# A two-layer attention kernel on one core: the last batch's stacks and rows of maxima on two queues, its value projections in the score banks

## The chip, the core and the metric

The kernel runs on 1 core of one Trainium2 chip. The metric is the device time in microseconds; lower is better. Engines are named as in the profile: PE (TensorE), DVE (VectorE), ACT (ScalarE), POOL (GpSimd), SP (SyncE, which here only issues DMAs). ACT issues DMAs too, from the same in-order list as its computations.

## The reference, cut to what matters

`x` is (16, 256, 512): 16 batches of 256 channels by 512 tokens. Two residual layers follow each other.

```python
def _L0_cond_ref(x, mask, Wq, Wo):             # 8 heads of 32, 512 tokens
    qh = heads(transpose(x) @ Wq.T)
    logits = (scale * qh @ qh^T * cmask + (1.0 - cmask) * NEG) * rmask
    ctx = softmax(logits) @ qh
    return transpose(ctx @ Wo.T)

def _L1_cond_ref(x, emb, W_emb, b_emb, g_norm, W_qkv, g_q, g_k, W_out):   # 16 heads of 32, 256 rows of 512
    scale, shift = split(emb @ W_emb + b_emb)
    xn = _rms_norm(x, g_norm) * (1.0 + scale) + shift
    q, k, v = split(xn @ W_qkv)
    q, k = _rms_norm(q, g_q), _rms_norm(k, g_k)
    o = softmax(q @ k^T * d ** (-0.5)) @ v
    return o + o @ W_out

x = x + _L0_cond_ref(x, cond, ...)
x = x + _L1_cond_ref(x, cond, ...)
```

## The kernel before

**The pipeline.** The program on each engine is a list of iterations, i = -1 to 17. A steady iteration does layer 0 of batch i (score steps A and B), layer 1 of batch i - 1 (steps C) and the output projection of batch i - 2. The engines meet by semaphores alone; on each engine the order is the one written out in the lists. Iterations 0 and 1, 15, 16 and 17 have lists of their own. **Iteration 16 is the one that the change touches**: no layer 0 is left there; it holds layer 1 of batch 15 and the output projection of batch 14 (`out1(i, i - 2, ...)`).

**Layer 1 of a batch, in its order.** `qk` (L598) projects queries and keys, `take_heads` and `square_heads` on ACT, `square_sums` and `add_eps` on DVE, `power_heads` on POOL (L2269) and `norm_heads` make the RMS norm. `heads_rows` (L616) transposes the heads on PE into four banks of PM. `round_heads` on ACT (L1317) rounds them to KQHI, `split1` on DVE (L1926) puts the remainder into KQLO and frees the bank. Scores are taken as a matmul over 97 rows: three stacked copies of 32 rows (high, low, high against high, high, low) and a row with the maxima. **A stack** is the six DMAs, 128 KB each, that copy these rows of one head of each group of four into A1 and B1 (`stack1_rows`); all of a stack's DMAs wait until the four banks are freed, so until `split1` 3. `maxima1` (L472) on PE and on DVE (L1826) find the maxima of 4 groups c = 0 to 3; in the last batch `rows1_half` transposes them in two halves on PE into PO (L488), ACT copies each half to NMT1 and issues four DMAs (L1281) that put them into row 96 of B1. `score1(c, h)` (L517), `exp1(c, h)` (L1217), `add_keys1` on POOL (L2287), `values_and_sums1(c)` (L552, L555), `take_context1`, `invert1` (L1934), `context1` (L1941) and `out1` (L632) follow; a score waits for the exponential two before it, since there are two score banks PS.

**Values.** `values1(i, t, ...)` (L598, V<-PX on ACT) projects the values of row block t. The argument list names the steps of the contraction, c = 0 to 3; each step is one product, two instructions in the trace, and the same holds for the steps of `out1`. Its result lies in PX, the bank of the order `BIG`, whose users wait for each other's evacuation by `big_taken`.

**The end of batch 14.** `out1(16, 14, t)` writes PX; `residual1` on DVE (L1947) adds PX to X1R and frees PX; `store` on SP (L2455) writes the two halves of X1R out (256 KB each, one after each residual). `keep_x1` on ACT copies X1, the residual of batch 15, into the same X1R. It waits for both stores:

```python
            def keep_x1(i, b):
                act.wait_ge(stored.sem, stored.at(b - 1))
                copy(X1R[:, :, :], X1[:, :, :]).then_inc(x1r_done.sem, 1)
```

In the list of ACT for iteration 16 `keep_x1` stands between `exp1(1, 3)` and `exp1(2, 0)`. In that of DVE `residual1(14, 0)` stands between `split1` 0 and `split1` 1, and `residual1(14, 1)` between the first and second `maxima1`. SP has stacks 0, 1 and 2, ACT has stack 3.

## Time and profile before

| | us |
|---|---|
| median of 3 runs | 1301.64 |
| lowest, highest | 1295.12, 1302.73 |
| the profiled execution | 1301.46 |
| its span | 1299.3 |
| mean granted clock of PE over the span | 0.974 |

The median is of separate executions; all rows are of the one profiled execution, whose span starts with its first instruction. The last batch's layer 1 takes the span's last 66 us, from about 1233 on.

### The profile page before, as it was taken

How to read it: one execution, taken by the hardware profiler on the slowest of the kernel's cores; microseconds unless marked ns; L12 is line 12 of the kernel's file. 1: busy time of each engine (PE TensorE's matmuls, PEld its weight loads, DVE VectorE, ACT ScalarE, POOL GpSimd, SP SyncE). 2: the span in 40 equal slices, each digit the busy share in tenths (PEclk: the TensorE clock that was granted, in tenths of full speed). 3: DMA queues.
4: the chain of work that ended last, by engine and by line, in shares of the span. 5: the costliest groups of instructions: out<-in, count | busy, mean ns of one | idle time of the engine just before them, and what ended most of it. 6: DMA issues, size and time to landing. Idle time of an engine off the chain costs nothing.

```text
span 1299.3 us, 20729 instructions
## 1 busy us (share of the span) xinstructions
PE 1239.1 (95%) x6769; PEld 579.9 (45%) x6769; DVE 1034.5 (80%) x920; ACT 768.6 (59%) x1394; POOL 770.4 (59%) x387
## 2 busy tenths in 40 slices
PE   6959899999999999999999999999999999999998
PEld 4314344544445454444545444454544444454434
DVE  5665878888887887888788788878878887887764
ACT  1525566665656666565666666566665656666623
POOL 1235648376665838666583866658385765837542
PEclk7778999999999999999999999999999999999999
DMA  7153543437354433636344363634336263433432
GB/s 211 38 191 90 114 115 81 108 85 169 83 134 108 107 102 92 160 82 139 105 102 107 94 157 82 147 98 104 103 100 150 83 152 93 112 99 72 103 70 60
DMA packets 77976, 143.00 MB, mean 110 GB/s; under 512 B 21553, under 2 KB 23089, under 8 KB 77873
## 3 DMA queue, kind: packets, MB, share of 16 engines
q1 hardware_dynamic: 69552, 130.36, 40.1%
q10 hardware_dynamic: 8320, 11.32, 3.3%
q8 instruction: 58, 0.95, 0.3%
q14 instruction: 46, 0.37, 0.1%
HBM read 32.02 MB, written 8.39 MB: 31 GB/s over the span
## 4 chain that ended last, share of the span: by engine, by line
PE 75%; POOL 7%; DVE 5%; SPq 4%; issue 4%; ACT 3%; DMA 1%; ACTq 1%; DVEq 0%; POOLq 0%
PE PX L598 24%; PE PS L500 8%; PE PO L530 7%; PE PX L632 7%; PE PS L517 5%; POOL RQK L2269 5%; PE PO L552 5%; SPq L2450 4%; PE PM L463 4%; PE PX L569 2%; PE PM L569 2%; PE PO L555 2%; PE PM L472 2%; PE PM L541 1%; PE PM L580 1%
## 5 line engine op out<-in xcount | busy, mean ns | idle before, releaser
L1210 ACT ACTIVATE E<-PS,KBIAS 128x512 f32<-128x512 f32 x512 | 340.8, 686 | 191.0 <-PE PS L500 150.0
L598 PE MATMUL PX<-WQKV,XNT 128*128 128x512 f32 x752 | 379.4, 607 | 1.3 <-ACT XNT L1354 0.8
L1819 DVE TENSOR_REDUCE NM<-PM 128x4 f32<-128x2048 f32 x128 | 292.0, 2282 | 73.9 <-PE PM L463 73.7
L2257 POOL TENSOR_TENSOR E<-E 128x1024 f32<-128x1024 f32 x112 | 262.8, 2366 | 95.8 <-PE PO L530 93.0
L500 PE MATMUL PS<-B,A 97*128 97x512 f32 x512 | 289.5, 600 | 3.4 <-ACT E L1210 2.7
L2287 POOL TENSOR_TENSOR KQLO<-E 128x1024 f32<-128x1024 f32 x64 | 151.5, 2368 | 227.3 <-ACT E L1217 225.7
L2269 POOL TENSOR_TENSOR RQK<-RQK,HALF 128x16 f32<-128x16 f32 x64 | 214.3, 3354 | 96.5 <-DVE RQK L1907 96.2
L1217 ACT ACTIVATE E<-PS 128x512 f32<-128x512 f32 x256 | 146.7, 597 | 111.5 <-PE PS L517 110.9
L598 PEld LDWEIGHTS PX<-WQKV,XNT 128*128 128x128 f32 x752 | 134.9, 192 | 99.3 <-issue 89.8
L1826 DVE TENSOR_REDUCE NM<-PM 128x8 f32<-128x2048 f32 x64 | 146.4, 2288 | 37.9 <-PE PM L472 37.9
L500 PEld LDWEIGHTS PS<-B,A 97*128 97x128 f32 x512 | 93.0, 191 | 158.1 <-issue 108.3
L517 PE MATMUL PS<-B,A 97*128 97x256 f32 x512 | 135.1, 371 | 5.2 <-ACT E L1217 2.5
L530 PE MATMUL PO<-E,V 128*32 128x512 f32 x1024 | 135.7, 613 | 1.4 <-ACT E L1210 1.4
L632 PE MATMUL PX<-WOUT,OT 128*128 128x512 f32 x248 | 126.3, 601 | 0.2 <-DVE OT L1941 0.2
L1934 DVE RECIPROCAL T<-T 128x256 f32<-128x256 f32 x64 | 111.5, 1742 | 12.1 <-ACT T L1188 12.1
L517 PEld LDWEIGHTS PS<-B,A 97*128 97x128 f32 x512 | 80.6, 190 | 82.4 <-issue 65.9
L1837 DVE TENSOR_TENSOR E<-E 128x1024 f32<-128x1024 f32 x80 | 102.8, 1286 | 16.9 <-ACT E L1210 15.4
L1857 DVE RECIPROCAL R<-R 128x256 f32<-128x256 f32 x64 | 109.6, 1735 | 1.0
L1188 ACT ACTIVATE QK<-PX 128x512 f32<-128x512 f32 x62 | 37.1, 599 | 75.7 <-PE PX L598 75.7
L463 PE MATMUL PM<-QHI 32*128 32x512 f32 x512 | 66.8, 510 | 13.0 <-DVE NM L1819 9.6
L1900 DVE TENSOR_REDUCE SSQ<-YSQ 128x16 f32<-128x512 f32 x64 | 43.7, 683 | 40.3 <-ACT YSQ L1301 40.3
L448 PE MATMUL PX<-XB,WQ 128*128 128x512 f32 x128 | 63.8, 622 | 7.2 <-DMA XB<-x 6.4
(87 smaller groups left out, 1354.6 us busy)
## 6 DMA issues: line engine op xcount, KB each, us to landing
A<-KQHI SPq DMA_DIRECT2D x126, 128.0 KB, 2.4
B<-KQHI SPq DMA_DIRECT2D x126, 128.0 KB, 2.5
A<-QHI SPq DMA_DIRECT2D x248, 64.0 KB, 2.0
B<-QHI SPq DMA_DIRECT2D x248, 64.0 KB, 2.0
XB<-x SPq DMA_DIRECT2D x16, 512.0 KB, 4.2
X<-x ACTq DMA_DIRECT2D x16, 512.0 KB, 5.0
out<-X1R SPq DMA_DIRECT2D x32, 256.0 KB, 2.9
A<-KQLO SPq DMA_DIRECT2D x63, 128.0 KB, 2.4
```

The costliest lines, as they stand in the source:

```text
L500: mm(PS[n % 2][:, :], A0[0:97, h, g * P:(g + 1) * P], B0[0:97, h, :], start=True, stop=True).then_inc(score_full, 1)
L517: last = mm(PS[n % 2][:, kb * N1:(kb + 1) * N1], A1[0:97, hq, c, kb * P:(kb + 1) * P], B1[0:97, hq, c, :], start=True, stop=True)
L530: last = mm(PO[h * DH:(h + 1) * DH, :], V0[:, q, g, h * DH:(h + 1) * DH], E[:, probs(seg, i, g), h, :], start=(g == 0), stop=(g == KB0 - 1))
L598: last = mm(bank, XNT[:, c, t * P:(t + 1) * P], WQKV[:, c, part * DM:(part + 1) * DM], start=(c == 0), stop=(c == 3))
L632: last = mm(bank, OT[:, c, t * P:(t + 1) * P], WOUT[:, c, :], start=(c == 0), stop=(c == 3))
L1210: fn(E[:, probs(seg, i, g), h, :], PS[n % 2][:, :], ACT.Exp, bias=KBIAS[:, g, b:b + 1], scale=SCALE).then_inc(exp_done, 1)
L1217: fn(E[:, probs("C", i, c), h, :], PS[n % 2][:, :], ACT.Exp, scale=SCALE_RAW).then_inc(exp_done, 1)
L1819: v.tensor_reduce(NM0[:, q, :].rearrange("p (h k) -> p h k", k=KB0)[:, :, kb], PM[:, :, :], axis=AX.X, op=ALU.max, negate=True).then_inc(m ...
L1826: v.tensor_reduce(maxima_rows(b)[:, c // 2, c % 2, :, :], PM[:, :, :].rearrange("p h (a k) -> p h a k", a=2), axis=AX.X, op=ALU.max, negat ...
L2257: g_.tensor_tensor(running(seg, i)[:, heads_, :], running(seg, i)[:, heads_, :], E[:, probs(seg, i, g), heads_, :], ALU.add).then_inc(done, 1)
L2269: g_.tensor_tensor(rqk, rqk, HALF[:, :], ALU.pow).then_inc(rqk_done.sem, 1)
L2287: g_.tensor_tensor(key_sums(c), e[:, :, 0:N1], e[:, :, N1:2 * N1], ALU.add).then_inc(esum_done.sem, 1)
```

## The change

It has four parts, all in iteration 16.

1. Stack 1 moves from SP to ACT: SP issues stacks 0 and 2, ACT stacks 1 and 3. Of the four DMAs of a half of the maxima (`half_rows`), ACT issues the first two and SP the last two, behind a wait for ACT's copy.
2. The value projections of batch 15 go to the banks of its first two scores (`last_values_bank`), which are free there; ACT counts their copies in a new semaphore `values_taken`, for which scores 0 and 1 and the first context wait. They leave the order `BIG`.
3. PE's list: value projections move forward, in between the transposes and the maxima; the steps of `out1(14, 0)` and `out1(14, 1)` move back behind them, the last two of `out1(14, 1)` in between the scores.
4. ACT's list takes both copies of V ahead of the first exponential and half 1 of the maxima behind the second; DVE's list takes `residual1(14, 1)` behind the fourth maxima.

```diff
         16: (
             (("p0", 0), 1, 0), (("p0", 1), 1, 0), (("w0", 0), 0, 0), (("p1", 0), -1, 0), (("p1", 2), -1, 0),
-            (("w1", 0), -2, 0), (("w1", 1), -2, 0), (("v1", 0), -1, 0), (("v1", 1), -1, 0)),
+            (("w1", 0), -2, 0), (("w1", 1), -2, 0)),
...
+        def half_rows(j):
+            return [(B1[96:97, h, 2 * j:2 * j + 2, :].rearrange("p c (k t) -> p (c k) t", t=P).bitcast(F32),
+                     NMT1[h * QH:(h + 1) * QH, j, :].bitcast(F32)) for h in range(QH)]
+
+        def last_values_bank(t):
+
+            return PS[SCORES.upto(("C", t), NB) % 2]
...
                 if b == NB - 1:
+                    if u < 2:
+                        pe.wait_ge(values_taken, u + 1)
...
                 if c == 0:
-                    pe.wait_ge(big_taken, BIG.upto(("v1", 1), i))
+                    if b == NB - 1:
+                        pe.wait_ge(values_taken, 2)
+                    else:
+                        pe.wait_ge(big_taken, BIG.upto(("v1", 1), i))
...
-                bank = heads_bank(i - 1, k) if key[0] == "p1" else PX[:, :]
+                late = key[0] == "v1" and i == NB
+                bank = last_values_bank(t)[:, :] if late else heads_bank(i - 1, k) if key[0] == "p1" else PX[:, :]
                 if cs[0] == 0:
-                    if key[0] == "p1" and i == NB and k % 2:
+                    if late:
+                        pe.wait_ge(exp_done, SCORES.ahead(("C", 0), i))
+                    elif key[0] == "p1" and i == NB and k % 2:
...
@@ PE, iteration_16
                 heads_rows(i, i - 1, 0)
                 heads_rows(i, i - 1, 1)
-                out1(i, i - 2, 0, 3)
+                values1(i, 0, 0)
                 heads_rows(i, i - 1, 2)
                 heads_rows(i, i - 1, 3)
-                out1(i, i - 2, 1, 0, 1)
+                out1(i, i - 2, 0, 3)
+                values1(i, 0, 1)
                 maxima1(i, i - 1, 0)
...
                 score1(i, i - 1, 1, 0)
                 score1(i, i - 1, 1, 1)
-                values1(i, 1, 1, 2, 3)
+                out1(i, i - 2, 1, 2)
                 score1(i, i - 1, 1, 2)
                 score1(i, i - 1, 1, 3)
+                out1(i, i - 2, 1, 3)
...
@@ ACT
-                for h in range(QH):
-                    act.dma_start(B1[96:97, h, 2 * j:2 * j + 2, :].rearrange("p c (k t) -> p (c k) t", t=P).bitcast(F32),
-                                  NMT1[h * QH:(h + 1) * QH, j, :].bitcast(F32)).then_inc(row1_half_in[j], 16)
+                for dst, src in half_rows(j)[:2]:
+                    act.dma_start(dst, src).then_inc(row1_half_in[j], 16)
...
                 round_heads(i, i - 1, 3)
+                stack1(i, i - 1, 1)
                 stack1(i, i - 1, 3)
                 rows1_half(i, i - 1, 0)
                 values1(i, i - 1, 0)
+                values1(i, i - 1, 1)
                 exp1(i, i - 1, 0, 0)
                 exp1(i, i - 1, 0, 1)
+                rows1_half(i, i - 1, 1)
                 exp1(i, i - 1, 0, 2)
                 exp1(i, i - 1, 0, 3)
-                rows1_half(i, i - 1, 1)
                 exp1(i, i - 1, 1, 0)
                 exp1(i, i - 1, 1, 1)
-                values1(i, i - 1, 1)
...
@@ DVE, iteration_16
                 maxima1(i, i - 1, 0)
-                residual1(i, i - 2, 1)
                 maxima1(i, i - 1, 1)
                 maxima1(i, i - 1, 2)
                 maxima1(i, i - 1, 3)
+                residual1(i, i - 2, 1)
...
@@ SP
+            def rows1_half(i, b, j):
+                sp.wait_ge(context_taken, CONTEXT_TAKEN.upto(("n1", j), i))
+                for dst, src in half_rows(j)[2:]:
+                    sp.dma_start(dst, src).then_inc(row1_half_in[j], 16)
...
             def iteration_16(i):
                 stack1(i, i - 1, 0)
-                stack1(i, i - 1, 1)
                 stack1(i, i - 1, 2)
+                rows1_half(i, i - 1, 0)
+                rows1_half(i, i - 1, 1)
                 store(i, i - 2)
```

What the lists become, at three places. Lines are those of each file; in the changed one `heads_rows` is L633, `out1` L649, `values1` L615, `maxima1` L481, `score1` L528, `rows1_half` L497 on PE.

PE from the second pair of head transposes to the first maxima, before:

```order
L616 MATMUL PM<-IDENT,QK 128x128 [waits bank_taken2,max_done,qn_done]
L616 MATMUL PM<-IDENT,QK 128x128 x3
L632 MATMUL PX<-WOUT,OT 128x512 [waits ot_done]
L616 MATMUL PM<-IDENT,QK 128x128 [waits bank_taken0,max_done,qn_done]
L616 MATMUL PM<-IDENT,QK 128x128 x3
L616 MATMUL PM<-IDENT,QK 128x128 [waits bank_taken1,max_done,qn_done]
L616 MATMUL PM<-IDENT,QK 128x128 x3
L632 MATMUL PX<-WOUT,OT 128x512 [waits ot_done,big_taken]
L632 MATMUL PX<-WOUT,OT 128x512 [waits ot_done]
L472 MATMUL PM<-KQHI 128x256 [waits bank_taken2,bank_taken3,bank_taken1,kqhi_done,bank_taken0,max_done]
L472 MATMUL PM<-KQHI 128x256 x7
```

and now:

```order
L633 MATMUL PM<-IDENT,QK 128x128 [waits bank_taken2,max_done,qn_done]
L633 MATMUL PM<-IDENT,QK 128x128 x3
L615 MATMUL PS1<-WQKV,XNT 128x512 [waits exp_done]
L633 MATMUL PM<-IDENT,QK 128x128 [waits bank_taken0,max_done,qn_done]
L633 MATMUL PM<-IDENT,QK 128x128 x3
L633 MATMUL PM<-IDENT,QK 128x128 [waits bank_taken1,max_done,qn_done]
L633 MATMUL PM<-IDENT,QK 128x128 x3
L649 MATMUL PX<-WOUT,OT 128x512 [waits ot_done]
L615 MATMUL PS1<-WQKV,XNT 128x512
L481 MATMUL PM<-KQHI 128x256 [waits bank_taken2,bank_taken3,bank_taken1,kqhi_done,bank_taken0,max_done]
L481 MATMUL PM<-KQHI 128x256 x7
```

The last step of `out1(14, 0)` stood ahead of the second pair of transposes and now stands behind it; a step of the values has its place.

PE at the second group of scores up to the first of the third, before:

```order
L517 MATMUL PS1<-B1,A1 128x256 [waits exp_done]
L517 MATMUL PS1<-B1,A1 128x256
L517 MATMUL PS0<-B1,A1 128x256 [waits exp_done]
L517 MATMUL PS0<-B1,A1 128x256
L598 MATMUL PX<-WQKV,XNT 128x512 x3
L517 MATMUL PS1<-B1,A1 128x256 [waits exp_done]
L517 MATMUL PS1<-B1,A1 128x256
L517 MATMUL PS0<-B1,A1 128x256 [waits exp_done]
L517 MATMUL PS0<-B1,A1 128x256
L517 MATMUL PS1<-B1,A1 128x256 [waits exp_done,row1_half_in1]
L517 MATMUL PS1<-B1,A1 128x256
```

and now:

```order
L528 MATMUL PS1<-B1,A1 128x256 [waits exp_done]
L528 MATMUL PS1<-B1,A1 128x256
L528 MATMUL PS0<-B1,A1 128x256 [waits exp_done]
L528 MATMUL PS0<-B1,A1 128x256
L649 MATMUL PX<-WOUT,OT 128x512 [waits ot_done]
L528 MATMUL PS1<-B1,A1 128x256 [waits exp_done]
L528 MATMUL PS1<-B1,A1 128x256
L528 MATMUL PS0<-B1,A1 128x256 [waits exp_done]
L528 MATMUL PS0<-B1,A1 128x256
L649 MATMUL PX<-WOUT,OT 128x512 [waits ot_done]
L528 MATMUL PS1<-B1,A1 128x256 [waits exp_done,row1_half_in1]
L528 MATMUL PS1<-B1,A1 128x256
```

The three steps of the values are gone from between the scores, and one step of `out1(14, 1)` stands behind the second score of the group, the last one behind the fourth.

ACT from stack 3 to the first exponentials, before:

```order
L1231 DMA A1<-KQHI 32x1024 [waits bank_taken1,bank_taken0,score_full,bank_taken2]
L1231 DMA A1<-KQLO 32x1024
L1231 DMA A1<-KQHI 32x1024
L1231 DMA B1<-KQHI 32x1024 x2
L1231 DMA B1<-KQLO 32x1024
L1188 ACTIVATE NMT1<-PO 16x128 [waits row1_in,n1_half0]
L1281 DMA B1<-NMT1 1x4x128 [waits context_taken]
L1281 DMA B1<-NMT1 1x4x128 x3
L1188 ACTIVATE V1<-PX 128x512 [waits visit_done,v1_full]
L1217 ACTIVATE E<-PS1 128x512 [waits score_full,visit_done]
L1217 ACTIVATE E<-PS0 128x512 [waits score_full]
```

and now, from the second DMA of stack 3, which has all of stack 1 ahead of it:

```order
L1253 DMA A1<-KQLO 32x1024
L1253 DMA A1<-KQHI 32x1024
L1253 DMA B1<-KQHI 32x1024 x2
L1253 DMA B1<-KQLO 32x1024
L1210 ACTIVATE NMT1<-PO 16x128 [waits row1_in,n1_half0]
L1303 DMA B1<-NMT1 1x4x128 [waits context_taken]
L1303 DMA B1<-NMT1 1x4x128
L1210 ACTIVATE V1<-PS1 128x512 [waits visit_done,v1_full]
L1210 ACTIVATE V1<-PS0 128x512 [waits visit_done,v1_full]
L1239 ACTIVATE E<-PS1 128x512 [waits score_full,visit_done]
L1239 ACTIVATE E<-PS0 128x512 [waits score_full]
```

The copy of the maxima's half 0 has six more DMA issues ahead of it, two instead of four behind it, and both copies of V are ahead of the first exponential.

## Rows read from the trace of the kernel before

**Rows 1.** The page: its header, and the chain's shares by engine.

```profile
span 1299.3 us, 20729 instructions
...
PE 75%; POOL 7%; DVE 5%; SPq 4%; issue 4%; ACT 3%; DMA 1%; ACTq 1%; DVEq 0%; POOLq 0%
```

**Rows 2.** The chain that ended last, in time: start us, us, what.

```profile
1256.25 0.51 SPq L2450
...
1267.85 3.68 DMA B<-KQLO
...
1295.27 0.87 PE PM L632 x2
1296.17 0.69 DVE X1R L1947
```

**Rows 3.** Timeline, 1251 to 1256: start, us, engine, line, operation, count [idle before].

```profile
1251.72 1.12 PE L632 MATMUL PX<-WOUT,OT 128*128 128x512 f32 x2 [0.18 <-DVE OT L1941]
...
1253.45 0.68 DVE L1947 TENSOR_TENSOR X1R<-PX,X1R 128x512 f32<-128x512 f32 x1
...
1254.04 2.06 DVE L1926 SCALAR_TENSOR_TENSOR KQLO<-PM,GQK,KQHI 128x512 fp32r<-128x512 f32 x3
...
1254.18 1.98 PE L632 MATMUL PX<-WOUT,OT 128*128 128x512 f32 x4
```

**Rows 4.** Timeline: the last issue of ACT's stack; the first of SP's second.

```profile
1259.89 0.69 ACTq L1231 DMA_DIRECT2D B<-KQLO  x1
...
1260.42 0.56 SPq L2450 DMA_DIRECT2D A<-KQHI  x1
```

**Rows 5.** Stretches: length, busy PE, PEld, DVE, ACT, POOL, PEclk, DMA share, GB/s.

```profile
1203.00:1209.00 6.00, 5.84 (x34) 2.19 (x26) 5.98 (x5) 3.21 (x5) 6.00 (x3) 1.00 0.92 201
...
1256.00:1258.00 2.00, 1.85 (x12) 1.01 (x12) 1.17 (x2) 0.00 (x0) 0.00 (x0) 1.00 0.33 66
1258.00:1260.00 2.00, 1.35 (x11) 0.42 (x10) 1.99 (x3) 0.00 (x0) 0.00 (x0) 1.00 0.97 275
1260.00:1262.00 2.00, 1.01 (x2) 0.18 (x2) 2.00 (x1) 0.00 (x0) 0.00 (x0) 0.99 1.07 246
1262.00:1264.00 2.00, 1.72 (x10) 1.12 (x11) 0.66 (x2) 0.27 (x1) 0.00 (x0) 0.50 1.05 219
...
1268.00:1270.00 2.00, 1.55 (x3) 0.48 (x4) 2.00 (x1) 0.57 (x1) 0.00 (x0) 0.80 1.03 235
...
1272.00:1274.00 2.00, 2.00 (x7) 0.99 (x5) 0.00 (x0) 1.22 (x3) 0.63 (x1) 0.55 0.07 15
```

**Rows 6.** DMA issues, median us to landing: batch 15's stacks (two), batch 14's (last).

```profile
A<-KQHI SPq DMA_DIRECT2D x6, 128.0 KB, 4.2
...
B<-KQLO ACTq DMA_DIRECT2D x1, 128.0 KB, 5.4
...
A<-KQHI SPq DMA_DIRECT2D x8, 128.0 KB, 2.4
```

**Rows 7.** Timeline of ACT, 1262 to 1282.

```profile
1262.98 3.06 ACTq L1281 DMA_DIRECT2D B<-NMT  x4
...
1273.09 0.25 ACT L1188 ACTIVATE NMT<-PO 16x128 fp32r<-16x128 f32 x1
1273.37 2.42 ACTq L1281 DMA_DIRECT2D B<-NMT  x4
1275.89 1.09 ACT L1217 ACTIVATE E<-PS 128x512 f32<-128x512 f32 x2 [2.55 <-PE PS L517]
...
1279.47 1.07 ACT L1188 ACTIVATE X1R<-X 128x1024 f32<-128x1024 f32 x1
1280.42 1.10 ACT L1217 ACTIVATE E<-PS 128x512 f32<-128x512 f32 x2
```

**Rows 8.** Timeline: PE's first scores, two scores of group 2, SP's last stores.

```profile
1269.84 0.71 PE L517 MATMUL PS<-B,A 97*128 97x256 f32 x4 [0.45 <-issue]
...
1279.26 0.90 PE L517 MATMUL PS<-B,A 97*128 97x256 f32 x4 [0.80 <-ACT E L1217]
...
1296.10 1.12 SPq L2455 DMA_DIRECT2D out<-X1R  x2
```

More of the change, by code:

```diff
@@ L363, in cond_resid @@
         big_taken = sem("big_taken")
+        values_taken = sem("values_taken")
         def running(seg, i):
@@ L433, in keep_warm @@
                 for _ in range(n):
-                    mm(PO[:, P:2 * P], IDENT[:, :], IDENT[:, :], start=True, stop=True)
+                    mm(PS[1][:, 0:P], IDENT[:, :], IDENT[:, :], start=True, stop=True)
             def quad_free(key, i):
@@ L1131, in iteration_16 @@
                 heads_rows(i, i - 1, 1)
-                out1(i, i - 2, 0, 3)
+                values1(i, 0, 0)
                 heads_rows(i, i - 1, 2)
                 heads_rows(i, i - 1, 3)
-                out1(i, i - 2, 1, 0, 1)
+                out1(i, i - 2, 0, 3)
+                values1(i, 0, 1)
                 maxima1(i, i - 1, 0)
-                out1(i, i - 2, 1, 2, 3)
+                values1(i, 0, 2)
+                values1(i, 0, 3)
                 maxima1(i, i - 1, 1)
-                values1(i, 0, 0)
+                values1(i, 1, 0)
+                values1(i, 1, 1)
                 rows1_half(i, i - 1, 0)
                 maxima1(i, i - 1, 2)
-                values1(i, 0, 1, 2)
+                values1(i, 1, 2)
+                values1(i, 1, 3)
+                out1(i, i - 2, 1, 0)
                 maxima1(i, i - 1, 3)
-                values1(i, 0, 3)
+                out1(i, i - 2, 1, 1)
                 score1(i, i - 1, 0, 0)
                 score1(i, i - 1, 0, 1)
+                rows1_half(i, i - 1, 1)
                 score1(i, i - 1, 0, 2)
                 score1(i, i - 1, 0, 3)
-                rows1_half(i, i - 1, 1)
-                values1(i, 1, 0)
                 score1(i, i - 1, 1, 0)
                 score1(i, i - 1, 1, 1)
-                values1(i, 1, 1, 2, 3)
+                out1(i, i - 2, 1, 2)
                 score1(i, i - 1, 1, 2)
                 score1(i, i - 1, 1, 3)
+                out1(i, i - 2, 1, 3)
                 score1(i, i - 1, 2, 0)
@@ L1305, in values1 @@
                 act.wait_ge(visit_done, visit("C", i - 1, 3) if b > 0 else 0)
-                copy(V1[:, t, :], PX[:, :]).then_inc(big_taken, 1)
+                if b == NB - 1:
+                    copy(V1[:, t, :], last_values_bank(t)[:, :]).then_inc(values_taken, 1)
+                else:
+                    copy(V1[:, t, :], PX[:, :]).then_inc(big_taken, 1)
             def round_heads(i, b, k):
@@ L1740, in iteration_16 @@
                 values1(i, i - 1, 0)
+                values1(i, i - 1, 1)
                 exp1(i, i - 1, 0, 0)
                 exp1(i, i - 1, 0, 1)
+                rows1_half(i, i - 1, 1)
                 exp1(i, i - 1, 0, 2)
                 exp1(i, i - 1, 0, 3)
-                rows1_half(i, i - 1, 1)
                 exp1(i, i - 1, 1, 0)
                 exp1(i, i - 1, 1, 1)
-                values1(i, i - 1, 1)
                 exp1(i, i - 1, 1, 2)
@@ L2526, in iteration_16 @@
                 stack1(i, i - 1, 0)
-                stack1(i, i - 1, 1)
                 stack1(i, i - 1, 2)
+                rows1_half(i, i - 1, 0)
+                rows1_half(i, i - 1, 1)
                 store(i, i - 2)
```

## The prediction

> **What bounds the kernel now.** The page comes first. Its header gives a span of 1299.3 us, and the chain that ended last goes through PE for 75% of it [rows 1]. So nearly everywhere a change has to shorten PE's own work to be worth much. This one touches only the last 45 us, where the last batch has nothing beside it, so the chain there, in order of time, comes next [rows 2]. The reader is to see the stacks: SP's issues begin at 1256.25, the last of the eighteen is followed by a landing that ends 3.68 us later, at 1271.53, and only behind it are all scores free. That stretch of 15.3 us is what the change is aimed at.
>
> Third, the timeline around 1251 to 1256 [rows 3] says what releases the stacks: the transposes of the heads on PE, then KQLO on DVE. Fourth, the two queues' issues, the table by stretches and the DMA answer [rows 4 to 6]: are the 15.3 us set by issuing or by the transfers? Fifth, ACT's rows from 1262 to 1282 [rows 7]: what stands ahead of each exponential. Last, PE's scores and the tail [rows 8], which holds a price needed below: how long it takes from the last output matmul to a landed store.
>
> **What the sum is made against.** The profiled execution took 1301.46 us for its span of 1299.3. That lies 0.18 us under the median of 1301.64, so a shift worked out on it is read as a shift of the median. The three runs spread from 1295.12 to 1302.73; a measurement of this kernel can tell about 1% (13 us) from no change.
>
> **Part 1: the output projection of batch 14, and what queues behind it on DVE.** Before, the last step of out1(14, 0) stands ahead of the second pair of transposes. It ran at 1251.72, in a gap in which PE waited for DVE anyway. DVE's first residual could then run at 1253.45, right behind split 0. Now a value projection has that gap, and the step stands behind the transposes. DVE's list keeps the residual between split 0 and splits 1 to 3, so the splits now wait for it. It starts where L632 started before at that place, 1254.18, and takes 1.12 us: 1255.30. The residual takes 0.68, the three splits 2.06: done at 1258.05 instead of 1256.10 [rows 3]. Both queues' stacks wait for the last split, and so do the maxima on PE. **The stacks start 1.95 us later.** Bounds: 0, if the residual came no later than at 1253.45; 3.1, if the step ran at half clock and took 1.12 more. I take 1.95; the clock there was 1.00.
>
> **Part 2: the stacks on two queues in equal parts.** Before: 18 issues on SP, 6 on ACT. Now 12 and 12. SP's first six take from 1256.25 to 1260.42; ACT's six ended at 1260.58 [rows 4]. At that pace twelve need some 8.5 us and end at 1266.7. But do the transfers follow? 24 DMAs of 128 KB (131,072 bytes) are 3.15 MB. In the six stretches of 2 us from 1258 to 1270 the DMA engines' share stands at 0.97 to 1.08 while they move 219 to 275 GB/s, mean 244 (first and last shown, with two between) [rows 5]. At that rate 3.15 MB are 12.9 us. In batch 14's stacks SP alone kept landings of 2.4 us, at a share of 0.92; here they are 4.2 on SP and 5.4 for the last of ACT's kind [rows 5, 6]. The issues are ahead of the transfers, not behind them. The share of 0.33 from 1256 to 1258 says that transfers began about 1.1 us after the first issue. So the last stack lands at 1258.2 + 1.1 + 12.9 = 1272.2, against 1271.53 before. Bounds: 1267.8, if landing follows issue (eleven issues at 0.65, then 2.4); 1273.5, if the old 15.3 us hold. I take 1272.2: the share is the nearest row.
>
> A rule of the Trainium skill speaks against this part: "Trainium Kernel Development and Optimization", section Key Constraints, says that the DMAs of SP's, ACT's and POOL's queues all run on the same 16 DMA engines, so that issuing from several engines saves only sequencer time. By that rule the stacks land at 1272.2, by issue time alone at 1267.8. The share near 1.0 agrees with the rule.
>
> **Part 3: the rows of maxima.** Before, ACT issued half 0's four DMAs at 1262.98, in 3.06 us [rows 7]. Now the copy that feeds them stands on ACT behind twelve stack issues, at 1266.7; SP's two DMAs wait for that copy. With two issues each they are out by 1268.5 and lie in the queues behind the stacks, so they land with the last stack. The first score, at 1269.84 before [rows 8], comes at about 1272.3, and all four heads are then ready at once. The two copies of V stand behind the issues on ACT; they have 3.8 us. DVE's four maxima start 1.95 us later too, lose the residual that stood between them, and end while the stacks still land.
>
> **Part 4: from the first score to the third group.** The value projections are gone from between the scores. They were part of the hold-up before: ACT waited 2.55 us for the second group's first score [rows 7]. In their place come two single steps of out1(14, 1). Walk from the first score at 0: first exponential at 0.45; two at 0.55 (a pair is 1.10) to 1.55; the copy of half 1, 0.25, and two issues, 1.2 (four took 2.42), to 3.0; two exponentials to 4.1. Score 1,1 needs the second of these and ends at 4.5; out1, 0.87, to 5.4; two scores at 0.45 to 6.3; the last out1 step to 7.1 [rows 2, 7, 8]. That is 1279.4 at full clock.
>
> **Part 5: the wait that is new.** ACT's copy of X1 into X1R waits until both halves of batch 14's store have landed, and it stands, unmoved, ahead of exponential 2,0. Before, out1(14, 1) was over ahead of the scores, and the copy ran at 1279.47 with no idle time [rows 7]. Now its last step stands behind score 1,3. From there a residual, an issue on SP and a landing have to pass. The tail shows exactly this chain: the last matmul ended at 1295.27 + 0.87 = 1296.14, then residual, issue and landing by the span's end, 1299.3: 3.15 us [rows 2, 8]. So the copy starts at 1279.4 + 3.15 = 1282.55 and exponential 2,0 at 0.95 more (1279.47 to 1280.42 before): 1283.5, against 1280.42, **3.1 us later**. Queued behind the copy on ACT are all remaining exponentials and contexts; PE's scores from 2,2 on and POOL's sums wait for those. PE's sums of context 0 get done under this wait, but that saves nothing, since their copy stands behind exponentials 2,0 and 2,1 on ACT.
>
> **The clock.** It stood at 0.50 from 1262, after stretches in which PE was busy 1.35 and 1.01 of 2 us, and at 0.55 from 1272 to 1274 [rows 5]. The new order leaves PE idle some 2 us before the first maxima and up to 3 before the first score. From score 1,1 to the last out1 step there are 3.1 us of PE on the path; at half clock they take 3.1 more. I take a third of it, 1.0, since the low stretch of before was short once the scores ran. Bounds 0 and 3.1.
>
> **Sum.** Part 5 contains parts 1 to 4: 3.1 + 1.0 = 4.1 us. 1301.46 + 4.1 = 1305.6; I say 1305.5. What follows exponential 2,0 stays as it is. The bounds of this case: +1.5 (last stack 0.6 earlier, full clock, a store landed in 2.1) to +7 (1273.5 and half clock).
>
> **Rivals.**
> *The transfers follow the issue (ends faster).* Place: the DMA queues from 1258 on. If two queues in equal parts get their stacks through as fast as they are issued, at 0.6 us each, issuing ends at 1265.4, the rows are out at 1266.9 and landed by 1268.5. Then 7.1 + 3.15 + 0.95 = 11.2 us lead to exponential 2,0 at 1279.7, 0.7 ahead of before: 1300.8. It decides from a first score earlier than 1269.2. For it: the issues of one queue, two thirds and more of them, stand on the chain [rows 2]. Against it: the share, and landings of up to 5.4 [rows 5, 6].
> *The clock stays low behind the wait.* PE stands idle for some 2.5 us ahead of score 2,2. If the next 6 us then run at half clock, with PE holding some 4 of them (it has 75% of the whole chain, rows 1), that is 4 more: 1309.6. For it: the falls near 1262 and 1272 both came where PE had waited. Against it: the tail's matmul at 0.87 us is of full length, though ACT and DVE made PE wait all through it.
> *Slow scores cover the store.* If only the DVE delay reaches the end, because the store's landing is covered in part, the end moves by the 0.7 of part 2 up to the 1.95 of part 1: 1302.8. For it: out1's steps find PE idle.
>
> **Chances.** Forecast 0.55, transfers follow the issue 0.2, low clock 0.1, cover 0.15. The forecast's own range is 1303 to 1308.5. The whole range has to hold most of the faster case and the scatter that a run at 1295.12 shows: 1299 to 1309. No case reaches 13 us either way: within 1% 0.96; faster by over 1% 0.01; slower 0.03, for scatter on top of the low clock.
>
> **What would show it.** Right: the last split of KQLO ends near 1258, with the X1R residual directly ahead of the three; the share stays near 1.0 until 1272; the first score (now line 528) starts at about 1272; ACT's copy into X1R has idle time of 2.5 to 3.5 us ahead of it, put down to a DMA of out; exponential 2,0 near 1283.5. Wrong: stacks landed before 1269, a copy into X1R without idle time, or splits done at 1256.

## The result and the profile after

| | before | after |
|---|---|---|
| median, us | 1298.52 | 1308.48 |
| lowest and highest, us (nine runs each) | 1295.12 to 1302.73 | 1304.56 to 1310.87 |
| ratio, 95% interval | | 1.0075 (1.0057 to 1.0092) |
| profiled execution, us | 1301.46 | 1306.72 |
| its span, us | 1299.3 | 1304.6 |

The change made the kernel 10.0 us slower by the medians. The time lies inside the stated range and inside 1%, with the sign that was forecast, but it is 3 us over the forecast time, and the loss is more than twice the 4.1 us that the sum gave. That the time still lies in the range is in part luck: the execution that the sum was made against lay 2.9 us above the median that nine runs gave, and this hides half of the 5.9 us by which the shift was missed.

The two profiles can't be compared by their spans. Whole executions of one kernel differ by up to 8 us (1295.12 to 1302.73 for before), and most of that arises before the work that was changed. In the timings that stand beside the experiments, before had medians of 1301.4 to 1303.0 and single executions from 1294.6 to 1309.9, so even the 10 us of the medians are less sure than the interval says. For this reason everything below is counted from a mark that both kernels have, the end of POOL's last power (RQK). From there to the end of the span is "the tail". It was 47.15 us before and 55.82 after. A second profile of each is among the experiments: 46.10 and 57.85. The means differ by 10.2 us, the first pair by 8.7. The mark lies 3.37 us earlier in the profile of after (1248.78) than in that of before (1252.15): add 3.37 to a time of after to set it beside one of before.

The chain of waits of after, in order of time (start us, us, what):

```profile
1245.40 3.38 POOL RQK L2294
...
1251.90 0.69 DVE X1R L1972
1252.59 1.99 DVE KQLO L1951 x3
1254.75 0.55 ACTq L1253
...
1267.19 1.34 ACTq L1253
1268.92 1.49 ACTq L1303
...
1271.66 0.60 ACT V L1210
1272.49 0.78 PE PS L528 x2
...
1280.50 1.72 PE PX L649 x2
1282.25 0.70 DVE X1R L1972
1282.97 2.01 DMA out<-X1R
...
1285.96 0.59 ACT E L1239
```

Against [rows 2]: the stacks' issues on the chain are ACT's now, not SP's. Behind them stand two row issues, a copy of V and the first score. The profile puts the score's wait down to the copy of V that ended last; the timeline of ACT below shows why that is not the whole of it. The last four rows are a chain that before had only at its very end: output matmul, residual, store, and an exponential behind it.

The timeline of after, DVE and the two queues (start, us, engine, line, operation, count, idle before), answers to [rows 3 and 4]:

```profile
1251.90 0.69 DVE L1972 TENSOR_TENSOR X1R<-PX,X1R 128x512 f32<-128x512 f32 x1 [1.74 <-PE PX L649]
1252.51 2.06 DVE L1951 SCALAR_TENSOR_TENSOR KQLO<-PM,GQK,KQHI 128x512 fp32r<-128x512 f32 x3
1254.71 0.51 SPq L2475 DMA_DIRECT2D A<-KQHI  x1
1256.56 2.57 SPq L2475 DMA_DIRECT2D B<-KQHI  x2
1257.20 2.65 ACTq L1253 DMA_DIRECT2D B<-KQHI  x2
```

The residual stands ahead of the three splits, and DVE waited 1.74 us for it. The B<-KQHI issues take 1.3 us each, where [rows 4] had 0.56 and 0.69. The same stretches as in [rows 5] (length, busy PE, PEld, DVE, ACT, POOL, granted clock, DMA share, GB/s):

```profile
1256.00:1258.00 2.00, 2.00 (x4) 0.67 (x2) 1.72 (x1) 0.00 (x0) 0.00 (x0) 0.50 1.02 205
1258.00:1260.00 2.00, 2.00 (x12) 0.79 (x11) 0.63 (x1) 0.00 (x0) 0.00 (x0) 0.79 0.98 197
1260.00:1262.00 2.00, 1.42 (x4) 0.28 (x2) 1.66 (x1) 0.00 (x0) 0.00 (x0) 1.00 1.00 199
...
1264.00:1266.00 2.00, 2.00 (x13) 0.86 (x12) 1.07 (x2) 0.00 (x0) 0.00 (x0) 1.00 1.03 244
...
1268.00:1270.00 2.00, 0.00 (x0) 0.00 (x0) 0.24 (x1) 0.27 (x1) 0.00 (x0) 0.77 1.00 203
1270.00:1272.00 2.00, 0.00 (x0) 0.00 (x0) 0.00 (x0) 0.84 (x2) 0.00 (x0) 0.50 0.42 86
...
1280.00:1282.00 2.00, 2.00 (x6) 0.97 (x4) 0.00 (x0) 1.09 (x2) 0.72 (x1) 0.50 0.00 0
```

The DMA engines' share is 1.0, as it was in [rows 5], but from 1256 to 1262 and from 1266 to 1270 they move 197 to 205 GB/s where they moved 219 to 275. Only in between, where one pair of stacks follows the other, do they reach 221 (1262 to 1264) and 244. The 3.15 MB took 15.0 us, a mean of some 210 GB/s. A share of 1.0 does not say at what rate. PE stood idle from 1268 to 1272, and its clock is 0.50 (the 1.2 GHz level) while the scores run. Last, the timeline of ACT and of PE's first scores, against [rows 7 and 8]:

```profile
1267.19 1.34 ACTq L1253 DMA_DIRECT2D B<-KQLO  x1
1268.63 0.27 ACT L1210 ACTIVATE NMT<-PO 16x128 fp32r<-16x128 f32 x1 [16.97 <-issue]
1268.92 2.13 ACTq L1303 DMA_DIRECT2D B<-NMT  x2
1271.16 1.09 ACT L1210 ACTIVATE V<-PS 128x512 f32<-128x512 f32 x2 [2.27 <-issue]
1272.49 1.19 PE L528 MATMUL PS<-B,A 97*128 97x256 f32 x4 [5.53 <-ACT V L1210]
...
1285.00 1.06 ACT L1210 ACTIVATE X1R<-X 128x1024 f32<-128x1024 f32 x1 [3.80 <-DMA out<-X1R]
1285.96 1.06 ACT L1239 ACTIVATE E<-PS 128x512 f32<-128x512 f32 x2
```

ACT's twelve issues reach from 1254.75 to 1268.53, and the rows of half 0 are issued behind them. The first score waits for three things: the stack, the first of the two copies of V (over at 1271.75) and the rows. By the semaphores' updates in the trace the last stack landed at 1271.53 and the last row at 1272.24, and the score started at 1272.49. The second copy of V, which it does not need, ended at 1272.25, and that is the one the profile names. So it was the rows that ended the wait. e2, described below, has the same issues and earlier copies of V (over at 1270.11), and there the profile names the rows:

```profile
1269.03 1.08 ACT L1210 ACTIVATE V<-PS 128x512 f32<-128x512 f32 x2 [2.17 <-issue]
...
1270.92 1.19 PE L528 MATMUL PS<-B,A 97*128 97x256 f32 x4 [6.49 <-DMA B<-NMT]
```

The copy into X1R, without idle time in [rows 7], now has 3.80 us ahead of it, put down to the store.

### The profile page after: what moved, and what is told of

It is laid out like the page before. It is cut to its first block, busy times and chain, and to the rows that moved or that the text cites. A ratio compares the mean times of both kernels' runs of the same rounds, so it can differ in the third digit from the quotient of the medians.

```text
span 1304.6 us, 20730 instructions
## 1 busy us (share of the span) xinstructions
PE 1237.2 (95%) x6769; PEld 580.1 (44%) x6769; DVE 1033.6 (79%) x920; ACT 767.5 (59%) x1394; POOL 769.7 (59%) x387
## 4 chain that ended last, share of the span: by engine, by line
PE 77%; POOL 7%; DVE 4%; issue 4%; ACT 3%; SPq 2%; ACTq 2%; DMA 1%; DVEq 0%; POOLq 0%
PE PX L615 24%; PE PS L509 9%; PE PO L541 7%; PE PX L649 7%; PE PS L528 5%; POOL RQK L2294 5%; PE PO L566 5%; PE PM L472 4%; PE PX L583 2%; SPq L2475 2%; PE PM L583 2%; PE PO L569 2%; PE PM L481 2%; PE PM L633 1%; PE PM L552 1%
## 5 line engine op out<-in xcount | busy, mean ns | idle before, releaser
L615 PE MATMUL PX<-WQKV,XNT 128*128 128x512 f32 x736 | 367.8, 602 | 1.0 <-ACT XNT L1378 0.6
L615 PEld LDWEIGHTS PX<-WQKV,XNT 128*128 128x128 f32 x736 | 131.1, 191 | 95.9 <-issue 86.9
L528 PE MATMUL PS<-B,A 97*128 97x256 f32 x512 | 137.8, 377 | 12.2 <-ACT V L1210 5.5
L649 PE MATMUL PX<-WOUT,OT 128*128 128x512 f32 x248 | 128.2, 607 | 0.0
L528 PEld LDWEIGHTS PS<-B,A 97*128 97x128 f32 x512 | 82.5, 194 | 89.8 <-issue 70.5
```

The costliest lines, as they stand in the source:

```text
L528: last = mm(PS[n % 2][:, kb * N1:(kb + 1) * N1], A1[0:97, hq, c, kb * P:(kb + 1) * P], B1[0:97, hq, c, :], start=True, stop=True)
L615: last = mm(bank, XNT[:, c, t * P:(t + 1) * P], WQKV[:, c, part * DM:(part + 1) * DM], start=(c == 0), stop=(c == 3))
L649: last = mm(bank, OT[:, c, t * P:(t + 1) * P], WOUT[:, c, :], start=(c == 0), stop=(c == 3))
```

## The experiments

Two theories. **Three costs**: the loss is made of the splits behind the residual, ACT's row of issues ahead of rows and values, and the copy into X1R that waits for a store. **Clock**: what counts is that PE stands idle and then runs at half clock. Each kernel is read by its tail, by where exponential 2,0 starts (counted from the mark), and by its timing against before. The table holds all twelve; the sections below say what each was.

| kernel | first exponential | exponential 2,0 | tail | ratio (95%) |
|---|---|---|---|---|
| before | 18.3 | 28.3 | 47.2 | |
| before again (e11) | 18.4 | 27.2 | 46.1 | |
| after | 24.6 | 37.2 | 55.8 | 1.0075 (1.0057 to 1.0092) |
| after again (e12) | 24.5 | 36.8 | 57.9 | |
| e1: X1R copied late | 24.6 | 33.2 | 52.5 | 1.0050 (1.0022 to 1.0077) |
| e2: residual behind splits | 22.4 | 34.4 | 55.5 | 1.0092 (1.0063 to 1.0121) |
| e3: issues as before | 20.3 | 33.3 | 54.5 | 1.0059 (1.0030 to 1.0088) |
| e4: 32 matmuls in PE's wait | 26.7 | 38.7 | 57.3 | 1.0086 (1.0054 to 1.0117) |
| e5: queues alone, on before | 22.6 | 33.5 | 52.4 | 1.0024 (0.9998 to 1.0050) |
| e6: e1, e2 and e3 together | 18.2 | 28.5 | 47.8 | 1.0002 (0.9978 to 1.0026) |
| e7: 14 matmuls in PE's wait | 24.2 | 35.8 | 55.8 | 1.0068 (1.0041 to 1.0095) |
| e8: e6, three row parts | 17.6 | 27.3 | 46.6 | 0.9989 (0.9965 to 1.0014) |
| e9: e5, other pairs of stacks | 21.7 | 31.3 | 50.2 | 1.0031 (0.9999 to 1.0062) |
| e10: e8 with 18 matmuls | 17.6 | 24.6 | 43.9 | 0.9971 (0.9946 to 0.9997) |

### One part undone at a time (e1, e2, e3)

**e1** moves ACT's copy into X1R, with its wait for the store, from ahead of exponential 2,0 to the end of ACT's exponentials:

```diff
                 exp1(i, i - 1, 1, 3)
-                keep_x1(i, i - 1)
                 exp1(i, i - 1, 2, 0)
...
                 exp1(i, i - 1, 3, 3)
+                keep_x1(i, i - 1)
                 take_context1(i, i - 1, 2)
```

> The changed kernel with ACT's copy of X1 into X1R moved from ahead of exponential 2,0 to ahead of the last context copy, so that nothing of the third group waits for batch 14's store. Measure: the tail, from the end of POOL's last L2269 (here L2294) to the end of the span; 47.1 us in the kernel before, 55.8 in the changed one. Theory (the store's landing is a wait of its own, after the last out1 step ends at 1282.2): exponential 2,0 comes 3 to 3.7 us earlier, tail 52 to 53, time some 3.5 us under the changed kernel's 1308.5. Rival (the slow scores and low clock set the pace of the third group anyway): tail 55 or more.

Timeline of ACT in e1 (exponentials 2,0 and 2,1, later the copy):

```profile
1281.63 1.08 ACT L1239 ACTIVATE E<-PS 128x512 f32<-128x512 f32 x2 [0.77 <-PE PS L528]
...
1288.14 1.05 ACT L1210 ACTIVATE X1R<-X 128x1024 f32<-128x1024 f32 x1
```

Exponential 2,0 comes 4.0 us earlier and the tail is 3.35 shorter, with the first exponential where it was. The copy finds the store landed. The new wait is real, and its price is the full one.

**e2** puts the first residual behind the splits on DVE:

```diff
                 split1(i, i - 1, 0)
-                residual1(i, i - 2, 0)
...
                 split1(i, i - 1, 3)
+                residual1(i, i - 2, 0)
```

> The changed kernel with DVE's first residual of batch 14 moved behind the last split of KQLO, so that the splits don't wait for the out1 step. Theory: the stacks start 1.9 us earlier against POOL's last power, and everything behind follows: tail 53.9. Rival (another wait, of the transposes' banks or of ACT's rounding, holds the splits, or the value projection in PX is held instead): tail 55 or more.

The stacks start 3.81 us behind the mark, not 5.93, the first exponential comes 2.2 earlier and exponential 2,0 2.75 earlier. That much came as expected, but the tail fell by only 0.3. From exponential 2,0 to the end this execution took 21.1 us where after took 18.6, with this stretch in it (columns as in [rows 5]):

```profile
1288.00:1290.00 2.00, 1.68 (x8) 1.39 (x6) 2.00 (x2) 1.43 (x4) 0.86 (x1) 0.50 0.00 0
```

A second stretch at 0.50, behind the wait for the store, took the gain back. The profile of after has none there. That of after again (e12) has one (its exponential 2,0 to the end took 21.1), and so has e3's. It comes and goes between executions of kernels that wait there. The timing of e2, 1.0092 from four executions, shows no gain over after at all, so what this part costs in the median is not settled by e2.

**e3** gives the issues back to SP as before, 18 and 6, and the rows to ACT:

```diff
@@ ACT
-                for dst, src in half_rows(j)[:2]:
+                for dst, src in half_rows(j):
...
-                stack1(i, i - 1, 1)
                 stack1(i, i - 1, 3)
@@ SP
                 stack1(i, i - 1, 0)
+                stack1(i, i - 1, 1)
                 stack1(i, i - 1, 2)
-                rows1_half(i, i - 1, 0)
-                rows1_half(i, i - 1, 1)
```

> The changed kernel with the issues as before: three stacks on SP, one on ACT, all rows of maxima on ACT; banks and PE order stay changed. Theory A (two queues in equal parts make each issue slower, 1.15 us against 0.65, and put the rows and the copies of V on ACT behind twelve issues): the first score comes 3 to 4 us earlier, tail 52 to 53. Theory B (the transfers alone set the pace, 12.9 us at 244 GB/s, whoever issues): last stack lands within 0.7 us of the same place, tail 55 to 56.

The first exponential comes 4.3 us earlier, as expected; exponential 2,0 3.8 earlier. The tail, 54.5, misses the expected 52 to 53 by the same low stretch (exponential 2,0 to the end 21.1). The timeline of e3: SP's two B<-KQHI of stack 0, and ACT's copy into X1R:

```profile
1262.80 1.51 SPq L2474 DMA_DIRECT2D B<-KQHI  x2
...
1287.41 1.06 ACT L1210 ACTIVATE X1R<-X 128x1024 f32<-128x1024 f32 x1 [3.21 <-DMA out<-X1R]
```

The two issues take 1.51 us where after's took 2.57 (in its timeline above), though in both kernels ACT issues a stack beside them. The wait for the store is still there, at 3.21. The intervals of e1, e2 and e3 all overlap that of after: taken one at a time, the costs show in the profiles and not in the timings.

### The clock alone (e4, e7)

**e4** fills PE's wait ahead of the first score with matmuls whose results nobody reads; **e7** is the same with 14. keep_warm(n) waits for the last maximum and multiplies the identity by itself n times into a bank that is then free:

```diff
                 out1(i, i - 2, 1, 1)
+                keep_warm(32)
                 score1(i, i - 1, 0, 0)
```

> The changed kernel with 32 extra matmuls of 128 columns on PE (into a bank of PM that nobody reads before it is written anew) between the fourth maxima and the first score, where PE is idle for 5.5 us. Theory (the idle stretch costs the clock, and the path from the first score at 1272.5 to the last out1 step at 1282.2 is 2.6 us longer than at full clock): granted clock 1.00 through the scores, tail 53 to 53.5. Rival (the path there is set by ACT and its issues): clock up, tail 55 or more; if the extra work delays the first score, tail over 56.

> As the run with 32 extra matmuls, with 14, since 32 took 7.4 us and held the first score up by 2.1; 14 take 3.3. Theory (the idle stretch costs the clock): clock 1.00 until the second group of scores, first score not later than in the changed kernel, tail 54 to 55 against 55.8. Rival (the clock falls all the same, or ACT sets the pace): tail 55.5 or more.

Timeline of PE in e4:

```profile
1264.67 7.41 PE L443 MATMUL PM<-IDENT 128*128 128x128 f32 x64 [1.33 <-DVE NM L1852]
1271.84 0.72 PE L528 MATMUL PS<-B,A 97*128 97x256 f32 x4
```

In e4 the 32 matmuls took 7.41 us, more than the wait, and held the first exponential up by 2.1; in e7 they took 3.39 and fitted. Both kept the clock at 1.00 over the first scores. Then it fell all the same. In e4 it stood at 0.77 from 1276 to 1278 and at 0.50 from 1278 to 1280. In e7 it fell at 1278.2, at the end of a wait of 1.60 us ahead of score 1,0, and again at 1288.5, behind a wait of 2.38 us. Two stretches of e7 in the low times, in which PE was busy throughout:

```profile
1279.00:1281.00 2.00, 2.00 (x6) 1.06 (x5) 0.00 (x0) 1.08 (x2) 2.00 (x1) 0.50 0.19 71
1289.00:1291.00 2.00, 2.00 (x21) 0.77 (x13) 1.90 (x2) 0.29 (x2) 1.75 (x1) 0.50 0.00 0
```

The tail of e7 is that of after. The clock by itself does not explain the loss: kept up at one place it fell at the next, as long as the waits were there.

### All three at once (e6)

> The changed kernel with all three costs taken out: old issues, the first residual behind the last split, the copy into X1R late. What is left of the change is the values in the score banks and PE's order. Theory (the three costs add up and explain the whole loss): first exponential 18.2 us after POOL's last power (20.3 of the run with old issues less 2.1), exponential 2,0 at 27.5, tail 46 to 47, so the time of the kernel before or just under it. Rival (the values' new place costs too, or the low clock takes the gain back): tail 48 or more.

e6 is after with the edits of e1, e2 and e3. What stays of the change is the new order of PE's list, the banks of the value projections, and the smaller moves on ACT (both copies of V early, half 1 behind the second exponential) and DVE (the second residual). First exponential 18.2, exponential 2,0 28.5, tail 47.8, ratio 1.0002. The three costs account for the loss. The single gains at exponential 2,0 are 4.0, 2.75 and 3.8, together 10.6; jointly they are 8.7, since each hides some of the others. The tail is just above the expected 46 to 47.

### The queues alone, and which stacks stand side by side (e5, e9)

**e5** is before with nothing but the issues of the change: SP stacks 0 and 2, ACT 1 and 3, twelve each, the rows two by two. **e9** is e5 with other partners, and nothing else changed:

```diff
@@ ACT
-                stack1(i, i - 1, 1)
                 stack1(i, i - 1, 3)
+                stack1(i, i - 1, 2)
@@ SP
                 stack1(i, i - 1, 0)
-                stack1(i, i - 1, 2)
+                stack1(i, i - 1, 1)
```

> The kernel before with the two queues alone: stacks 0 and 2 on SP, 1 and 3 on ACT, each half of the maxima's rows 2 and 2; nothing else moved. Tail: 47.1 us in the kernel before. Theory (issues of both queues back up behind the transfers, 12 of them take 13.8 us instead of 8.5, and ACT's rows and its copy of V stand behind them): each of the later issues 1.0 to 1.3 us, first exponential 21 to 22 us after POOL's last power instead of 18.3, tail 49 to 50. Rival (the equal parts are good by themselves, and only the moved out1 and residual cost): first exponential at 18 or earlier, tail 46 to 47.

> The kernel before with the queues in equal parts, as in the run with the queues alone, but paired otherwise: SP issues stacks 0 and 1, ACT 3 and 2, instead of 0 and 2 beside 1 and 3. Reason: in the kernel before, six issues on SP (stack 0) and six on ACT (stack 3) ran side by side at 0.70 us each and 275 GB/s; with stacks 0 and 1 side by side the fourth issue on either queue took 1.3 us and the transfers ran at 200 GB/s. Theory A (which source partitions stand side by side decides): the first six issues of each queue take 4.2 us as before, 250 GB/s or more there; 12 issues in 8.5 to 11 us, tail 2 to 3 us under the 52.4 of the other pairing. Theory B (two full queues slow each other, whatever they carry): 1.15 us an issue again, tail 51.5 to 53.

Timelines of both queues in e5 (stack 0 on SP beside 1 on ACT), and a stretch of it:

```profile
1262.43 2.57 SPq L2454 DMA_DIRECT2D B<-KQHI  x2
1263.06 2.67 ACTq L1235 DMA_DIRECT2D B<-KQHI  x2
```

```profile
1262.90:1264.90 2.00, 1.36 (x11) 0.60 (x10) 1.98 (x3) 0.00 (x0) 0.00 (x0) 1.00 0.99 197
```

The same in e9 (0 beside 3), with ACT's last issue and the first exponential, and a later stretch:

```profile
1259.11 1.51 SPq L2454 DMA_DIRECT2D B<-KQHI  x2
1259.40 1.52 ACTq L1235 DMA_DIRECT2D B<-KQHI  x2
...
1265.32 0.62 ACTq L1235 DMA_DIRECT2D B<-KQLO  x1
...
1274.91 1.09 ACT L1221 ACTIVATE E<-PS 128x512 f32<-128x512 f32 x2 [5.81 <-PE PS L521]
```

```profile
1259.40:1261.40 2.00, 1.36 (x10) 0.60 (x10) 1.98 (x3) 0.00 (x0) 0.00 (x0) 1.00 1.02 264
1262.00:1264.00 2.00, 0.65 (x10) 0.42 (x9) 1.17 (x1) 0.00 (x0) 0.00 (x0) 1.00 1.08 221
```

Same queues, same instructions, same bytes, share 1.0 in both, and 197 against 264 GB/s in the first full stretch. ACT's twelve issues take 13.8 us in e5 and 8.6 in e9. Over the whole of the stacks the difference is smaller: e5 moves 197 to 207 GB/s and once 262, e9 201 to 229 behind its first stretch. From the first issue to the last landing e5 takes 16.8 us (1260.58 to 1277.35), e9 15.95 (1257.29 to 1273.24) and before 15.3, so the partners explain about half of what the equal parts add.

A stack reads the 32 partitions of its head. Stacks 0 and 1 read partitions 0 to 31 and 32 to 63, 2 and 3 those from 64 on; the slow pairs are 0|1 and 2|3, the quick ones 0|3 and 1|2. The prediction did not weigh this. The Trainium skill, "SBUF — State Buffer", section "Door 1: The DMA port swizzle", has a rule that fits in part: partitions 0 to 63 reach the same 8 of SBUF's 16 DMA ports as 0 to 31, and the other 8 are those of 64 to 127; its asymptote for 8 ports is some 218 GB/s. The 197 to 207 GB/s of the slow pairs lie under it, the 264 of 0|3 over it. Not all rows agree. In before SP issued stack 1 by itself. ACT's last stack DMA had landed at 1265.28, and the six of stack 1 landed from 1265.60 to 1268.34, five of them within 2.74 us. That is 239 GB/s out of partitions 32 to 63 alone; this stretch, which has the start of stack 2 in it at most at its end, gives as much:

```profile
1266.00:1268.00 2.00, 2.00 (x11) 0.71 (x10) 0.08 (x1) 0.00 (x0) 0.00 (x0) 0.50 1.08 253
```

The Trainium skill also says, on the same page under "Can I just issue two DMAs to hit both halves?", that two at once, one in each half, gain only 6% over a single one. No run here has a single one beside them; partners from both halves gave 34% over partners from one half in the first full stretch (264 against 197) and about 9% over the whole (3.15 MB in 13.8 us against 15.0). That the partners matter is shown; that ports are the mechanism is an inference with a row against it, since only the pairs were tried.

Even so e9 keeps a tail of 50.2, against 46 to 47. With quick stacks the rows still stand behind twelve issues on both queues; the first score comes at 1274.04. Its line puts the idle time down to issue, but by the semaphores' updates in the trace the last row landed at 1273.95, right before it and 0.7 us behind the last stack (1273.24). It is the same 0.7 in after (1272.24 against 1271.53) and in e5 (1278.07 against 1277.35). In before, where the rows had only six issues ahead of them on ACT, they landed at 1269.75, 1.8 ahead of the last stack.

e5's tail of 52.4 missed the expected 49 to 50. Its first exponential, at 22.6, is 0.6 later than expected, and from there to exponential 2,0 it takes 10.9 us where before took 10.0, at a clock of 0.50 for most of the way, which the expectation left out.

In the timings the two are within 0.3% of before and of each other: 1.0024 and 1.0031, neither interval free of 1. That the pair matters is shown at the issues and the transfers and by a first exponential 0.9 us earlier (which repeated within 0.1 us in before and after). It is not shown in the medians, and the tails' difference of 2.2 is hardly more than the 2.0 by which two profiles of one kernel differ.

### What is to be had (e8, e10)

**e8** is e6 with the rows shared two by two, but half 0's rows on SP between its second and third stack. **e10** adds matmuls nobody reads to e8, in the two places where PE waits: eight behind the copies of V, into a score bank, and ten behind the last maximum, into a bank of PM:

```diff
+                keep_warm(8, 0)
                 score1(i, i - 1, 0, 0)
                 score1(i, i - 1, 0, 1)
                 rows1_half(i, i - 1, 1)
+                keep_warm(0, 10)
                 score1(i, i - 1, 0, 2)
```

> The run with the three costs taken out, with one part of the change back: of each half of the maxima's rows, SP issues two (half 0 between its second and third stack) and ACT two. Theory (two issues fewer on ACT between exponentials 0,1 and 0,2 are worth their 1.0 to 1.2 us, without a queue of stacks ahead of them): tail 1.0 shorter than in that run. Rival (PE or the stack's landing ends last there): no difference over 0.3.

> The run with the three costs taken out and the rows on two queues, with 8 extra matmuls of 128 columns ahead of the first score and 10 ahead of score 0,2, in the 2.0 and 2.7 us in which PE waits for DMAs there (32 took 7.4 us). Nobody reads what they write. Theory (the low clock from 1267 to 1275 of that run costs 1.5 to 2.5 us on the path of the second group): clock 1.00 there, tail 44.5 to 45.2 against 46.6. Rival (the low stretch only moves to a later place, as with 14 matmuls): tail 46 to 47.

Timeline of PE in e8 at the first scores:

```profile
1265.49 0.71 PE L528 MATMUL PS<-B,A 97*128 97x256 f32 x4 [2.04 <-DMA B<-NMT]
...
1268.98 1.22 PE L528 MATMUL PS<-B,A 97*128 97x256 f32 x4 [2.67 <-DMA B<-KQLO]
```

Timeline of e10, the fillers on PE and exponential 2,0 on ACT; then the stretch of its first scores, and one of e8 for comparison:

```profile
1270.00 1.95 PE L444 MATMUL PS<-IDENT 128*128 128x128 f32 x16
1272.83 2.39 PE L448 MATMUL PM<-IDENT 128*128 128x128 f32 x20
...
1279.74 1.09 ACT L1246 ACTIVATE E<-PS 128x512 f32<-128x512 f32 x2 [0.31 <-PE PS L533]
```

```profile
1275.10:1277.10 2.00, 1.55 (x11) 1.16 (x10) 0.00 (x0) 1.38 (x3) 0.29 (x1) 1.00 0.21 79
```

```profile
1271.10:1273.10 2.00, 2.00 (x6) 1.11 (x5) 0.00 (x0) 1.09 (x2) 2.00 (x1) 0.50 0.00 0
```

e8's tail is 1.2 us shorter than e6's, where 1.0 was expected; that is within what two profiles of one kernel differ by. e8 leaves PE two waits of 2.0 and 2.7 us, both for DMAs. Filled, the clock stays at 1.00, where e8's scores ran at 0.50 (the two stretches lie 20 and 23 us behind their marks). The first exponential does not move (17.6), exponential 2,0 comes 2.8 earlier, the tail is 2.7 shorter. The fillers that did nothing in e7 work here, where the longest wait behind them, up to exponential 2,1, is 0.45 us; e7 had 1.60 and 2.38. The kernels differ in more than that, so this is the likely reason and not a shown one. e10's ratio of 0.9971 (0.9946 to 0.9997) is under 1 by little. The interval of after lies wholly above it: this version beats after, and before by a margin at the edge of what was measured, as one of ten versions timed.

### The scatter (e11, e12)

> The kernel before, profiled once more, to see how far the tail of one execution scatters while whole executions differ by up to 15 us. If the tail is a fair measure of the last batch: 47.1 within 0.5 us. If the low clock falls elsewhere by chance: up to 2.5 us away, and single tails tell no less than that apart.

> The changed kernel, profiled once more, for the same reason: 55.8 within 0.5 us if the tail is a fair measure; up to 2.5 us away if the low clock moves by chance, above all behind the store's landing, where three of the other runs had a second low stretch and the changed kernel's first profile had none.

The mark lay at 1245.0 in before again and at 1254.9 in after again, the other way round than in the first profiles, while the tails repeated within 1.1 and 2.0 us. The 2.0 are the second stretch at 0.50:

```profile
1295.00:1297.00 2.00, 1.68 (x9) 1.27 (x6) 1.95 (x2) 1.59 (x3) 1.63 (x1) 0.50 0.00 0
```

## Why the prediction was right in sign and too small

**Part 1, the splits behind the residual: right.** The stacks start 1.83 us later behind the mark (5.93 against 4.10); 1.95 was said. e2 takes it back. Its reach to the end was not shown in a timing.

**Part 2, the stacks: the step that failed.** From the first issue to the last landing 14.0 us were said (1258.2 to 1272.2); it took 16.8 (1254.71 to 1271.53). Transfers began 1.1 us behind the first issue, as said. They took 15.0 us where the sum had 12.9, and the last landing came 0.7 behind their end, which the sum had at nothing. The rate of 244 GB/s, "the share is the nearest row", is the mean of stretches with a quick pair and of SP alone; the change moved some 210. e9, with the same bytes in quick pairs, took 13.8 us: 1.2 of the missing 2.1 us are the partners, and why e9 still stays under 244 (its mean is 229) is open. "At that pace twelve need some 8.5 us" took the issue pace of stack 0 beside stack 3 from [rows 4] and used it for 0 beside 1; it measured 13.8 us, and 8.6 in e9. The last stack so landed 22.8 us behind the mark where 20.1 were said. The rule of the Trainium skill that the prediction named, that all queues share one pool of DMA engines ("Trainium Kernel Development and Optimization", section Key Constraints), agrees with the share near 1.0 and says nothing of the rate.

**Part 3, the rows: right in what is waited for, too early.** The prediction had the rows in the queues behind the stacks, landing with the last one, and the first score behind the last landing. That is what happened, but the first score came 23.7 us behind the mark (1272.49), where 20.2 were said: 2.7 from part 2, and the rest since the rows land 0.7 behind the last stack and the score starts 0.25 behind them. ACT's issues were to be out by 1266.7, 14.6 us behind the mark of before; they were out at 1268.53, 19.8 behind that of after. "They have 3.8 us" was said of the copies of V; they had 1.2, from the last row issue (over at 1271.06) to the landing of the rows, and took 1.09. That they did not cost more is a near thing. e3 moves the first exponential by 4.3.

**Part 4, from the first score to the last output step: right walk, clock under-sized.** Said 7.1 and 1.0 for the clock; measured 9.7 (1272.49 to 1282.22). The granted clock was 0.50 throughout, so the term was 2.6, near its bound of 3.1. e10 against e8, which differ by the fillers alone, agrees: from the first exponential to exponential 2,0 it is 7.0 us at 1.00 against 9.8 at mostly 0.50. The share of a third was the wrong choice: the longer wait of part 3 stood ahead of it.

**Part 5, the store: right.** Said 3.15 from the last output step to the copy and 0.95 more, 4.1; measured 3.7 from 1282.22 to 1285.96. e1 removes it and gets 4.0 at exponential 2,0 and 3.35 at the end.

**The sum.** Exponential 2,0 came 8.9 us later behind the mark (37.2 against 28.3), against 4.1: 3.5 more from parts 2 and 3 and 1.6 more from the clock, less 0.4 in part 5. The tails' means differ by 10.2; what lies between that and 8.9 is the second stretch at half clock of some executions.

**The rivals.** Transfers that follow the issue fell: e9's issues took 8.6 us, where that rival wanted 7.2, and still its last stack landed 7.3 us behind the last issue's end, with the first exponential late. Cover for the store fell with e1. The low clock behind the wait is real in some executions (e2, e3, e7 and e12; about 2.4 us each in e2, e3 and e12, from exponential 2,0 to the end) and absent in after's first profile. It belongs to the loss as part of its scatter, and its share of the median is open.

## What to carry to other kernels

When DMAs are spread over two queues, look at which partitions the neighbours in time read, and pair those of the lower half with those of the upper (here twelve issues took 8.6 us instead of 13.8, and the last landing came 0.8 us sooner; the medians did not show it). A DMA share of 1.0 is not a rate, so read the GB/s beside it. An engine that issues DMAs can't do its copies until the issues are through, and small transfers issued behind large ones land behind them: put what the next stage needs ahead of them. Where an instruction waits for several things, check the one that the profile names against what the code waits for. A wait for a store belongs where nothing is queued behind it.

## What the runs showed of the chip beyond this

- An issue's own duration follows the partners: from the fourth on 0.9 to 1.35 us with partners 0|1 and 2|3 (but for one of 0.62 in e5), and 0.5 to 0.9 with 0|3 or 1|2, on both SP and ACT.
- The granted clock stood at 0.50 in stretches in which PE was busy all the time (1279 to 1281 and 1289 to 1291 in e7: 2.00 of 2.00 us), behind waits of 1.60 and 2.38 us. Fillers in one wait moved the fall; fillers in both waits of e8 kept 1.00.
- Half 0's rows, DMAs of 2 KB, landed 0.4 to 0.7 us behind the last stack in all eight profiles in which they were issued behind twelve stack DMAs on each queue (after, e12, e1, e2, e4, e5, e7, e9), whatever the rate of the stacks.
- Nothing changed in the first 1240 us, and yet the mark lay anywhere from 1245.0 to 1256.5 in the fourteen profiles. With effects of 3 us that hides everything in a span, and little in the stretch behind the mark.
